# A scratch tensor with its two halves side by side, and one more product a step in a later stage

## What is computed

```python
xn = _layernorm(x)
h = (xn @ W.T).reshape(n, 8, 32)
h_src, h_dst = h[src], h[dst]
alpha = sum(h_src * a_src) + sum(h_dst * a_dst)
alpha = leaky(alpha + sum(relu(edge_attr @ edge_W.T + edge_b) * h_dst))
attn = softmax of alpha over the edges of one destination
x = x + segment_sum(h_src * attn, dst) + bias + linear_attention(xn)
x = x + sum over e of w[:, e] * expert_e(_layernorm(x))
```

## Time and profile before

| what | us |
|---|---|
| median of 3 runs | 4826.66 |
| lowest and highest | 4821.68, 4843.91 |
| the profiled execution | 4848.34 |
| its span, first to last instruction | 4846.5 |
| first stage | about 190 |
| edge stage | about 2665 |
| combination | about 123 |
| mean granted TensorE clock over the span | 0.872 |

### The profile page before, as it was taken

One profiled execution on the slowest core, in us unless ns is written; L12 is line 12 of the kernel. 1 busy time (PEld: TensorE's weight loads), 2 busy tenths in 40 slices (PEclk: granted clock), 3 DMA queues, 4 the chain that ended last, 5 costly groups with the idle time before them and its releaser, 6 DMA issues. The chain is left out here.

```text
span 4846.5 us, 80424 instructions
## 1 busy us (share of the span) xinstructions
PE 4087.7 (84%) x22764; PEld 1897.1 (39%) x22765; DVE 2700.2 (56%) x5470; ACT 2291.3 (47%) x6074; POOL 1780.1 (37%) x1859
## 2 busy tenths in 40 slices
PE   5699988957888887788887878878887999999999
PEld 3333322312333333333333333333333666666666
DVE  7566723336666666676666666667666333333333
ACT  4444445524555555555555555555554433333332
POOL 3255555644454445444444444445440000000000
PEclk8799989976888888888888887888887799999999
DMA  7555556655555555555555555555552100000000
GB/s 216 160 165 162 164 177 201 210 156 154 161 168 165 158 165 164 162 168 168 159 162 152 163 157 161 162 159 168 164 162 67 61 8 1 8 8 8 8 8 8
DMA packets 378173, 629.74 MB, mean 130 GB/s; under 512 B 83912, under 2 KB 245063, under 8 KB 377536
## 3 DMA queue, kind: packets, MB, share of 16 engines
q1 hardware_dynamic: 277266, 356.80, 23.4%
q0 software_dynamic: 93408, 257.23, 19.5%
q10 hardware_dynamic: 7104, 11.01, 0.7%
HBM read 520.59 MB, written 104.12 MB: 129 GB/s over the span
## 5 line engine op out<-in xcount | busy, mean ns | idle before, releaser
L1629 POOL DMA_INDIRECT s_rows<-scratch_src_rows,s_idx_w x1312 | 1257.6, 959 | 1367.6 <-PE s_ps_a L1692 563.3
L1837 DVE SCALAR_TENSOR_TENSOR s_enc<-s_enc,s_a_dst,s_ps_d 128x512 f32<-128x512 f32 x904 | 634.9, 741 | 313.3 <-DMA p_feats<-in_edge_f,p_tcol_i 160.8
L1734 ACT ACTIVATE s_enc<-s_ps_f 128x1024 f32<-128x1024 f32 x452 | 459.5, 1017 | 516.6 <-remote 265.5
L1692 PE MATMUL s_ps_a<-s_rows,s_hot_e 128*64 128x264 f32 x3616 | 647.1, 490 | 44.9 <-DVE s_rows L1920 32.4
L2285 DVE SCALAR_TENSOR_TENSOR kx_y_all<-e_ps_o,kx_gate,kx_y_all 128x256 f32 (+1 forms) x392 | 173.5, 480 | 684.2 <-PE e_ps_o L2340 684.2
L1920 DVE TENSOR_TENSOR s_rows<-s_rows,s_ps_x 128x1024 f32<-128x1024 f32 x452 | 545.7, 1207 | 13.6 <-ACT s_a_w L1765 8.7
L1688 PE MATMUL s_ps_a<-ke_sums,k_ident 128*128 x790 | 341.0, 520 | 217.1 <-DVE ke_sums L1913 123.6
L1913 DVE TENSOR_TENSOR ke_sums<-s_ps_a,ke_sums 128x264 f32 x509 | 218.3, 429 | 505.3 <-remote 263.9
L1669 PE MATMUL s_ps_s<-s_enc,s_head_sum 128*32 128x256 f32 x3616 | 353.7, 469 | 152.9 <-DVE s_enc L1837 121.2
L1779 ACT ACTIVATE s_hot_e<-k_iota_row,s_rel_w 128x64 f32<-128x64 f32 x1808 | 480.5, 339 | 0.0
L1787 ACT COPY ke_sums<-s_ps_a 128x264 f32 x395 | 148.6, 376 | 552.5 <-remote 337.8
(11 more groups left out here) (280 smaller groups left out, 5259.0 us busy)
## 6 DMA issues: line engine op xcount, KB each, us to landing
s_table<-scratch_dst_parts SPq DMA_DIRECT2D x904, 96.0 KB
s_rows<-scratch_pre_rows SPq DMA_DIRECT2D x124, 528.0 KB
s_relb<-scratch_rel_rows SPq DMA_DIRECT2D x226, 256.0 KB
scratch_pre_rows<-n_rows SPq DMA_DIRECT2D x62, 528.0 KB
scratch_pre_rows<-m_rows SPq DMA_DIRECT2D x62, 528.0 KB
s_rows<-scratch_src_rows,s_idx_w POOLq DMA_INDIRECT x1312
s_feat<-scratch_step_parts SPq DMA_DIRECT2D x226, 54.0 KB
s_pen_w<-scratch_pen_rows SPq DMA_DIRECT2D x228, 48.1 KB
```

The costliest lines, as they stand in the source:

```text
L1629: pool.indirect_dma_start(out=rows[:, d % R, m, :], out_offset=None, in_=scr["src_table"], in_offset=bass.IndirectOffsetOnAxis(ap=idx_w[:, ...
L1692: last = PE.matmul(ps_a[t * WN:(t + 1) * WN, sub, 0:SRC_W], hot_e[:, d % 3, 2 * sub + t, :], rows[:, d % R, 2 * sub + t, :], start=(sub == ...
L1734: A.activation(enc[:, d % 2], ps_f[:], ACT.Relu).then_inc(enc_made, 1)
L1837: V.scalar_tensor_tensor(out=enc[:, d % 2, c, :], in0=enc[:, d % 2, c, :], scalar=a_dst[:, c:c + 1], in1=ps_d[:, c, :], op0=ALU.add, op1=A ...
```

## The change

Three edits. The scratch tensor `dst_parts` is laid out as block, node, half, column instead of block, half, node, column. So a tile of `parts` is stored by one transfer of 128 lines of 768 numbers instead of two of 64 x 2 x 384, and the counts of `d_stored` go by 16 instead of 32. The load of `table` brings back the old order in SBUF: half by half, its source is 2 x 64 x 384 with a step of 384 between halves and 768 between nodes. In `stage_combine` TensorE multiplies the identity with 256 columns of `keep["spare"]` into a new bank `ps_w` in each of its 70 steps, and four times with 512 columns ahead of them; nobody reads `ps_w`. The wait for `w_in` moves to the step in which the first transposes come.

```diff
                         sp.wait_ge(part2, d + 1)
-                        for b in range(2):
-                            sp.dma_start(scr["dst_parts"][2 * d + b].rearrange("c n w -> n c w"), parts[b * WN:(b + 1) * WN, d % RP]).then_inc(d_stored[d % RP], 16)
+                        sp.dma_start(scr["dst_parts"][2 * d:2 * d + 2].rearrange("b n c w -> (b n) (c w)"), parts[:, d % RP].rearrange("p c w -> p (c w)")).then_inc(d_stored[d % RP], 16)
...
-                    sp.wait_ge(d_stored[u], 32 * len(range(u, NT, RP)))
+                    sp.wait_ge(d_stored[u], 16 * len(range(u, NT, RP)))
...
-                    wait(act, d_stored[u], 32 * (i // RP))
+                    wait(act, d_stored[u], 16 * (i // RP))
...
-                        sp.dma_start(table[:, u, sub, :], row(scr["dst_parts"], j).rearrange("o c n w -> (o c n) w")).then_inc(table_in[u], 16)
+                        sp.dma_start(table[:, u, sub, :], row(scr["dst_parts"], j).rearrange("o n c w -> c (o n) w")).then_inc(table_in[u], 16)
...
+        ps_w = s.ps("ps_w", [P, 512])
...
+                def keep_busy(columns):
+                    PE.matmul(ps_w[:, 0:columns], keep["ident"][:], keep["spare"][:, 0:columns], start=True, stop=True)
+
+                for _ in range(4):
+                    keep_busy(2 * C)
                 pe.wait_ge(band_in, 16)
-                pe.wait_ge(w_in, 32)
                 for i in range(NT + LATE + 2):
+                    if i == LATE:
+                        pe.wait_ge(w_in, 32)
+                    keep_busy(C)
...
-        src_rows=dram("src_rows", (NT, P, SRC_W)), dst_parts=dram("dst_parts", (NJ, 2, WN, HALF), BF16),
+        src_rows=dram("src_rows", (NT, P, SRC_W)), dst_parts=dram("dst_parts", (NJ, WN, 2, HALF), BF16),
```

## The result

The changed kernel takes 5306.0 us (median of 3 runs, 5292.7 to 5310.4), the kernel before 4826.7 us. The ratio is 1.095, with a 95% interval of 1.091 to 1.099. The forecast was 5445 us with a range of 5000 to 6080, so direction and range hold, and the size is 139 us too high.

What follows compares the result with a forecast made beforehand. SyncE's issues were taken to pace the first stage, with no engine full in the edge stage. Terms -30 + 650 + 0 = +620 gave 5468 us against the profiled execution, 5445 in the median's terms; range 5000 to 6080.

Steps and rivals of the forecast that it cites:

- First stage: Stores of `p_parts`: 98 issues become 49 on SyncE's queue, which sets the pace; -30 us, bounds 10 and 50 us gained.
- Two engines: Edge stage: each changed table load, with outermost counts 2 and 128, goes through two DMA engines instead of 16.
- One sign: Edge stage, profile after: TensorE or VectorE now waits for `s_table` by name.
- the load's term: Edge stage: table loads through two DMA engines make it 3250 us, 7.2 us a step, +650 us.
- sum of durations: Edge stage, estimate from above: packet durations on each of the two engines sum to 3837 us, +1235.
- The bound by bytes: Edge stage, estimate from below: bytes at the fastest stretch's rate per engine give 2821 us, +219.
- SyncE's dearer issue: Edge stage: two table loads cost SyncE +0.5 to +0.9 us a step, costed at nothing; without cover at most 400 us.
- rival 1: Edge stage: the new load still goes through many engines, no cost from four on; 4797 us in all, chance 0.12.
- The combination: Added identity products and later wait: -10 us with the clock held, +27 without; taken as 0.
- Durations right or worse: Edge stage: two engines, a stage of 3837 us or more, 6030 us and above; chance 0.18 for above 5850.
- rate of the bytes: Edge stage: two engines at the bytes' rate, stage 2821 us, total 5015 us; chance 0.10 for 4950 to 5150.
- The store does nothing: First stage: one 128-line issue takes as long as two, or DMA engines cause the stalls; costs 20 us of the gain.

Runs made afterwards that it cites:

- its later group: The changed kernel itself, run again as an anchor beside later experiments: 5271.5 us against 4781.9 for the unchanged kernel, ratio 1.103.
- the spare line: Unchanged kernel with one spare line behind each half in the scratch tensor, so the table load's source is 2 x 64 lines: 5152.5 us, ratio 1.288.
- four pieces: Unchanged kernel with the table's source in four pieces of 32 lines plus a spare line each, four stores a tile: ratio 1.031; again at 4.0 ms level 1.113.
- the experiment on `s_feat`: Changed kernel with `s_feat` loaded by three transfers of 9 lines instead of one of 3 x 9: 5164.2 us against 5271.5 for the changed kernel.
- the kernel with products alone: Unchanged kernel with only the combination's edits, identity products and later wait: 4005.8 us against 3999.2, ratio 1.0002.
- The later wait alone: Unchanged kernel with the later wait, no products, and one of a tile's two stores issued by ScalarE: 3982.0 us against 3999.3, ratio 0.9953.

## Why the prediction was right, and where its sizes were off

**First stage: right.** -30 was said. The stage ends at 167.3 instead of 190.1 us (-22.8; "near 160" was said), and the first table load comes 27.5 us earlier; the other 4.7 us fall in stages that the change doesn't touch. The 49 issues are shorter than the 0.61 us assumed; 29.4 us of ScalarE's wait stay, so the upper bound of -50 was rightly not taken.

```profile
L357 SPq DMA_DIRECT2D scratch_dst_parts<-p_parts x49: 337/451/2932, 42.0 to 162.7; - x49
...
ACT p_parts L514 <- DMA scratch_dst_parts<-p_parts: 29.4, 11, 8.2
```

In its later group the changed kernel's first stage ended at 168 us, against 187 to 191 for kernels with two stores in any group.

**Two engines: right**, by the 2 small packets of a load, by the spare line that brings the same step without the interleaving, and by four pieces that bring 4. The rule of the Trainium skill ("DMA: Bandwidth & Descriptors", section "Why a DMA increments its semaphore by 16 and not by 1"), the largest k up to 16 that divides both slowest counts, agrees at 2 and at 4, counts that the trace of before didn't have. Its sentence that SyncE's queue takes the lowest-numbered k engines agrees with the experiment on `s_feat` in so far as the engines are shared: -107 us. No row names an engine, so the numbers themselves are not shown.

**One sign did not come.** TensorE or VectorE was to wait for `s_table` by name; it is 5.9 us, and the named wait is that for `s_feat`, 409 us. TensorE's share of the stage was to fall to some 0.65 and is 0.75, since its products took 230 us more at the lower clock.

**The size of the load's term: +650 said, +481 measured.** This is the step that was mis-sized, in two factors, both in the sum of durations. It took 5.64 us of engine time a load from one stretch, which is 44 ns a packet; over the edge stage the table packets of the changed kernel have a mean of 37.6 ns. With it, and with all other transfers taken as spread evenly over the engines, which no row shows, the sum for one of the two engines is 904 x 64 x 37.6 ns = 2175 us, 1131 us of all other transfers (45.5% of 3083, less the tables' 272) and 141 us of `s_feat`: 3447 us in a stage that lasted 3083. The overlap is thus 1.12 by this estimate, where the highest DMA share of the trace, 1.05, had been used. 44 to 37.6 ns takes 375 us off the 3837, and 1.05 to 1.12 about 200 more. The bound by bytes, 2821 us, was too low by 262 us, so the choice half way between was the right kind of answer and too high by 5%. A mean from hundreds of packets was to be had in the trace of before (41.2 ns in its edge stage); one stretch of 144 was taken instead. It would have taken off 166 of the 375 us; that the mean would fall further, to 37.6, no row of before could tell.

**SyncE's dearer issue at nothing: right here, for the reason given, and wrong in size.** The step became longer than SyncE needs, so the two engines hide it. But +0.5 to +0.9 us a step counted only the DMA instruction, and that part is +0.54; the read of the block's number behind it grows too, and the whole is +1.17 us a step. Where the cover is gone, with four engines, it cost +417 us of stage at the 4.0 ms level and some 120 at the other. "At most 400 us" was near, by luck: a term was missing, and waits that shrank made up for it. It also corrects rival 1: "from four engines on nothing is left of the cost" is false. Four engines cost 3.1% in all at the 4.8 ms level and 11.3% at the other. A load of such a form through all 16 engines was not tried, so how much of SyncE's price it would have kept stays open.

**The combination: 0 said, -8 measured, and both kinds of end seen.** From the last table load to the experts it is 177.7 us in the changed kernel against 186.0, and 178.0 and 178.4 in two other runs with products. There the clock held to the end. In the kernel with products alone it was 195.9:

```profile
2862.00:2886.00 24.00, 24.00 (x121) 9.66 (x119) 22.21 (x103) 3.85 (x9) 0.00 (x0) 1.00 0.70 209
2886.00:2910.00 24.00, 23.43 (x152) 13.89 (x148) 17.28 (x79) 8.29 (x22) 0.00 (x0) 1.00 0.00 1
2910.00:2942.00 32.00, 30.85 (x199) 18.27 (x198) 21.29 (x98) 15.26 (x38) 0.00 (x0) 1.00 0.00 1
2942.00:2987.00 45.00, 38.22 (x167) 32.08 (x167) 9.17 (x37) 16.82 (x42) 0.00 (x0) 0.63 0.47 164
```

Full clock for 80 us as in the changed kernel, then a mean of 0.63 in the last stretch, which took 45 us instead of 33. In all that is 9 us more than the 186.9 of the unchanged kernel at that level. Of the seven profiled kernels with these products three fell back to half clock at the end (187.8, 194.2 and 195.9 us), one had a dip (185.9), and three held it (177.7 to 178.4); the seven without them took 181.7 to 190.6. So the -8 is what this kernel got and not what the products give. Why the clock fell in some kernels and not in others stays open. The later wait alone gave 5 us without any product, in one profile each.

**The rivals.** "Durations right or worse" (above 5850 us) and "rate of the bytes" (5015 us) were both off; the truth lay between them and nearer the bytes. "Many engines" fell. "The store does nothing" fell, by issues of 0.45 us and a stage 22.8 us shorter.

**Not foreseen at all:** the size of the price depends on what the step was before, because two full engines are a ceiling at 6.8 us a step. At the 4.8 ms level this is +9.5%, and at the 4.0 ms level +28%.

## What to carry to other kernels

Before you change a layout for the sake of its stores, write down the outermost counts of every transfer on both sides, and compare the busiest DMA engine with the step, not the mean of sixteen: 904 loads lost here what 49 stores gained, seventeen times over (480.6 us against 27.5). Count what a load costs the issuing engine from start to start, with the instructions behind it. Look at the issue time of an unrelated DMA in the same queue: here it was 1.92 us where the transfers were the bound, and 0.43 to 0.58 where they weren't. Where issues of one queue are too many, give some to another engine's queue before touching the shape of the data: with 49 stores that shortened the first stage by 13.7 us here, and the edge stage kept its 4.22 us a step.

## What was not expected of the hardware

The unchanged kernel took 4782 us in one group and 3991 in another on the same chip. In its profiles at the two levels, which are of other groups, DMA packets have nearly the same mean duration (41.2 and 40.7 ns for a table packet). So the level is not a property of the chip, as the expectations above have it. The operations of SyncE itself differ. The register operation ahead of a table load, first in the kernel before at 4.8 ms, then in the unchanged kernel at 4.0 ms (ns min/median/max):

```profile
L1600 SPq FUSED_REGOPS  x904: 2/42/801, 1038.2 to 3640.5; - x181
```

```profile
L1600 SPq FUSED_REGOPS  x904: 42/42/48, 886.2 to 2796.7; - x181
```

One takes between 2 and 801 ns, the other never more than 48. In front of the products of line 948, in an earlier stage, TensorE sat 152.8 us on its issue in the first and 43.5 in the second, and in the edge stage it had a granted clock of 0.81 and of 0.95. I read this as gaps in the engines' own instruction streams at the upper level, whose slack hid most of the price of the change; no run separates it from other causes. What makes the level was not tried and stays open.

A load of 128 lines whose two sides have unlike shapes cost SyncE 0.62 us instead of 0.34, and the read of a number from SBUF behind it 0.735 us instead of 0.268. A transfer of 64 plain lines cost 0.47 us, and the read stayed at 0.269. By the estimate above, two DMA engines that are the bound got through 1.12 us of packet durations in 1 us of time.
